# Moving the start of every large SBUF tile to a multiple of 256 bytes

## The chip, the cores and the metric

The kernel runs on one core of one Trainium2 chip. The metric is the device time of one execution in microseconds (us); lower is better. The core has a matrix engine (TensorE, PE in the rows), three elementwise engines (VectorE = DVE, ScalarE = ACT, GpSimd = POOL), an engine that here issues most transfers (SyncE = SP), and 16 DMA engines between HBM and the on-chip memory SBUF. SBUF has 128 partitions; a tile takes the same byte range in each of them, and "where a tile begins" below is its byte offset in the partition.

## The reference

A gated block on x of [8, 512, 512], in float32. A cut version:

```
xn  = layer_norm(layernorm(x)) * gamma;  ctx = layer_norm(ctx_1024) * ctx_gamma
q   = xn @ Wq (16 heads of 64);  k, v = ctx @ Wkv (one head for all)
att = softmax(where(mask == 0, -inf, q k^T / 8)) v @ Wout
ff  = (silu(xn @ Wff1[gate]) * (xn @ Wff1[a])) @ Wff2
x   = x + tanh(g_xattn) * (att + ff)
y   = layernorm(x)
o   = slot_query + attention(slot_query -> y)            # 16 slots per batch
o   = o + expert_e(layer_norm(o))                        # 16 experts, one slot each
x   = x + tanh(g_ffn) * attention(y -> o)
```

## The kernel before

The products that need precision are split. A float32 tile is kept as a high part (rounded to the matrix engine's fp32r type) and a low part (the rest), and a product is three matrix multiplies: high x high, high x low, low x high (`products`). So nearly every large multiply has the form 128x128 stationary weights, 128x512 moving rows, 512 result columns in one PSUM bank.

The program has five stages, one after the other, each with its own SBUF plan:

1. `cross_attention`, from the start to about 600 us. For each batch `b` of 8 and each pair of heads `i` of 8, TensorE runs `pair_scores(b, i)` (L619, L622), the next batch's `queries(b+1, i)` (L580, 12 multiplies), `maxima` (L598) and `pair_out(b, i)` (L632, L633, L636). At the end of each batch come the output projections `output` (L652). ScalarE makes the exponentials (`prob_hi`, `prob`), VectorE their low part (`prob_lo`, L971), GpSimd splits the finished heads (`oT_hi`, `oT_lo`).
2. `feed_forward`, to about 1650 us: `ff_up` (L1384) and `ff_down` (L1444), weights in `w1_*` and `w2_*`, rows in `ff_b*`, `ff_t*`, `u*`.
3. `slot_attention`, to about 1790 us. `score` (L2030) multiplies `A` by `yT`; `sums` (L2051) multiplies the turned probabilities `pT` by the normalised rows `yn`. Even batches use `pT_hi_even` and `pT_lo_even`, odd ones `pT_hi_odd` and `pT_lo_odd`.
4. `experts`, to about 2245 us: 16 experts' weights of 12 MiB each are streamed from HBM.
5. `token_attention`, to the end (`c_scores` L2820, `c_out` L2853).

The order of the instructions on each engine is the order in which the code issues them; there is no scheduler. SBUF places come from the order of the `mem.sbuf` calls: each tile begins where the one before it ends, so one small tile shifts all that follow. Two tiles of `gated_block`, `ident` and `gates`, and the one-number tile `many`, live for the whole program and lie below all stages. Some tiles are reserved under a plan of one stage and used by the next, so the plans must agree on every offset; that is why the filler `slot_filler` of `slot_attention` is computed from `used`, the bytes taken so far.

Which multiply takes which tile as weights is given by the order of the arguments:

```python
for w, m in products((wq_hi, wq_lo), (nT_hi, nT_lo)):                  # queries, L580
    matmul(bank[:, :], w[:, k, i * P:(i + 1) * P], m[:, k, :], ...)    # weights, moving rows
for n, (o, w) in enumerate(products((oT_hi, oT_lo), (wo_hi, wo_lo))):  # output, L652
    matmul(banks[t], o[:, i, t * P:(t + 1) * P], w[:, i, :], ...)
for a, m in products([x[...] for x in pT[b % 2]], [x[...] for x in yn]):   # sums, L2051
```

Every slice in these lines starts a multiple of 256 bytes behind its tile's start, so its position within 256 bytes is that of the tile.

Of the kernel before, what the change touches and what calls it, by code (L numbers as in the profile page):

```python
# [5 lines left out]
F32R = mybir.dt.float32r  # L6
# [5 lines left out]
P = 128  # L12
B, S, D = 8, 512, 512
KT = D // P
TT = S // P
# [4 lines left out]
SH, SD = 16, 32  # L20
HS = SH * NS
EPS = 1e-5
MASKED = -1e30


# [11 lines left out]
class Memory:  # L37
# [5 lines left out]
    def sbuf(self, name, shape, dtype=F32):  # L43
        return self.stage.enter_context(self.nc.sbuf_tensor(name, shape, dtype))
# [79 lines left out]
def several_blocks(nc, whole, taken, I, ident, gates, x1_d, x1_out_of_first, x1_stores):  # L124

    with ExitStack() as stage:
# [139 lines left out]
        def vector(dve):  # L266
# [3 lines left out]
            with dve.Fori(0, B) as b:  # L270
# [6 lines left out]
                rows_mean_var(nc, stats[:, :, :], mean[:, :], var[:, :], spread[:, :])  # L277
                nc.vector.tensor_scalar(spread[:, 0:TT], var[:, 0:TT], EPS, None, ALU.add)
                nc.vector.tensor_scalar(spread[:, TT:2 * TT], var[:, TT:2 * TT], 1 + EPS, EPS * EPS, ALU.mult, ALU.add).then_inc(dve_step, 1)
                after(dve, act_step, A + 1)  # L280
# [34 lines left out]
def cross_attention(nc, whole, taken, I, ident, gates, many, first, x1_d, xnT_d, t_d, PIECES):  # L315
# [4 lines left out]
    with ExitStack() as stage:  # L320
        mem = Memory(nc, stage, whole, taken)
# [13 lines left out]
        minus = mem.sbuf("minus", [P, P], F32R)  # L335
        first_bias = mem.sbuf("first_bias", [P, B])
        start = mem.sbuf("start", [1, B], I32)
        ones = mem.sbuf("att_ones", [1, P])
        live, dead = mem.sbuf("live", [P, P]), mem.sbuf("dead", [P, P])
        mask_i = live[:, :].bitcast(I32)  # L340
        inv_count, k_sum = (mem.sbuf(n, [P, 1]) for n in ("inv_count", "k_sum"))
# [3 lines left out]
        mv = mem.sbuf("mean_var", [P, ROWS, 2])  # L345
        spread, rstd = (mem.sbuf(n, [P, ROWS]) for n in ("spread", "rstd"))
        mean = lambda n: mv[:, n, 0:1]

        xin = mem.sbuf("xin", [P, TT, D])
        craw = mem.sbuf("craw", [P, D])  # L350
# [9 lines left out]
        q_hi = mem.sbuf("q_hi", [P, HP, S], F32R)  # L360
        q_lo = mem.sbuf("q_lo", [P, HP, S], F32R)
        MC = DH + HP
        m_rows = mem.sbuf("m_rows", [P, TT, MC])
        m_heads = mem.sbuf("m_heads", [P, S], F32R)
        prob = mem.sbuf("prob", [P, 2, S])
        prob_hi = mem.sbuf("prob_hi", [P, 2, S], F32R)
        prob_lo = mem.sbuf("prob_lo", [P, 2, S], F32R)
        inv = mem.sbuf("inv", [P, 2, S])
# [6 lines left out]
        SC, MX, OB = (pair_bank(n) for n in ("att_scores", "att_maxima", "att_out"))  # L375
# [14 lines left out]
        live_f, rank, from_end, is_first = (flag_place[:, i * B * TT:(i + 1) * B * TT].rearrange("o (b j) -> o b j", j=TT) for i in range(4))  # L390
        best, begin, several = (flag_place[:, 4 * B * TT + i * B:4 * B * TT + (i + 1) * B] for i in range(3))
        flat = lambda ap: ap.rearrange("o b j -> o (b j)")

        first_in = [mem.sem(f"first_in{t}") for t in range(2)]
        x_in, c_in, mask_in, masks_in = (mem.sem(n) for n in ("x_in", "c_in", "mask_in", "masks_in"))
# [4 lines left out]
        ident_ready, consts, bias_ready, flags_turned, firsts_ready, firsts_spread, start_ready = (  # L400
            mem.sem(n) for n in ("ident_ready", "consts", "bias_ready", "flags_turned", "firsts_ready", "firsts_spread", "start_ready"))
# [33 lines left out]
        with nc.Block() as block:  # L435
# [85 lines left out]
            def _(pe):  # L521
# [144 lines left out]
                nc.tensor.matmul(OB[0:1, 1, 0:B * TT], live_col, ident[0:B * TT, 0:B * TT], start=True, stop=True).then_inc(flags_turned, 1)  # L666
                turn_first()
                pe.wait_ge(firsts_ready, 1)
                nc.tensor.matmul(OB[:, 1, 0:B * TT], ones[:, :], flat(is_first), start=True, stop=True).then_inc(firsts_spread, 1)
                for i in range(3):  # L670
                    queries(0, i)
                turn_context(0)
# [220 lines left out]
            def _(dve):  # L893
# [10 lines left out]
                def variances(rows):  # L904
# [5 lines left out]
                    if rows[0] == 0:  # L910
                        last = nc.vector.tensor_scalar(spread[:, 0:1], var(0, 1), EPS, None, ALU.add)
                    if rows[-1] == ROWS - 1:
                        last = nc.vector.tensor_scalar(spread[:, 1:ROWS], var(1, ROWS), 1 + EPS, EPS * EPS, ALU.mult, ALU.add)
                    last.then_inc(var_ready, 1)
# [70 lines left out]
                        nc.vector.scalar_tensor_tensor(x_rows[:, t, :], out_banks(b)[t], gates[:, 0:1], x_rows[:, t, :],  # L985
                                                       ALU.mult, ALU.add).then_inc(x_added, 1)

                nc.vector.memset(ones[:, :], 1.0)
                def split_wq(k):
                    dve.wait_ge(wq_hi_done, k + 1)  # L990
                    nc.vector.tensor_tensor(wq_lo[:, k, :], raw_wq[k], plain(wq_hi[:, k, :]), ALU.subtract).then_inc(wq_lo_dve, 1)
# [815 lines left out]
def slot_attention(nc, whole, I, ident, x_stats, slot_w, weights_in, wo_in, xin, x_in, vectors, small_in, ff, x1_stored, ff_down, low_bytes, o2T, hT, x1_d, yT_d):  # L1807

    with ExitStack() as stage:
        mem = Memory(nc, stage, whole)  # L1810
# [19 lines left out]
        shift, top, nb, total, mv, *inv = (columns[:, 2 * i:2 * i + 2] for i in (0, 1, 2, 3, 5, 4, 10))  # L1830
        last_rstd, spare_col = columns[:, 22:23], columns[:, 30:31]
        sd, bv_col, stat1 = columns[:, 12:13], columns[:, 16:16 + KT], columns[:, 24:30]
        used = 4 * (B * TT * 6 + 4 * KT * D + P + 4 * B * TT + 32)
        second_pT = [mem.sbuf(f"pT_{part}_even", [P, TT, HS], F32R) for part in ("hi", "lo")]
        mem.sbuf("slot_filler", [P, (low_bytes - used) // 4 - 2 * TT * HS])

# [60 lines left out]
        flat = lambda t, i: t[:, 2 * i:2 * i + 2, :].rearrange("p t n -> p (t n)")  # L1897
# [271 lines left out]
        def statistics(first, last):  # L2169
            part = slice(first, last)  # L2170
            rows_mean_var(nc, x_stats[:, part, :], mean[:, part], var[:, part], half[:, part])
            nc.vector.tensor_scalar(var[:, part], var[:, part], EPS, None, ALU.add).then_inc(kept, 1)

# [55 lines left out]
        def vector(dve):  # L2229
# [62 lines left out]
            nc.vector.drain()  # L2292
            nc.vector.tensor_scalar(sd, mv[:, 1:2], EPS, None, ALU.add).then_inc(kept, 1)
            nc.vector.scalar_tensor_tensor(h_in[:, :], o1[:, :], mv[:, 0:1], e_gain[:, :], ALU.subtract, ALU.mult)
# [759 lines left out]
def gated_block(nc, I, out):  # L3054

    scratch = lambda name, shape: nc.dram_tensor(name, shape, F32, kind="Internal").ap()
    x1_d = scratch("x1", [B, S, D])
    xnT_d = scratch("xnT", [2, B, P, KT, S])
    t_d = scratch("ff_t_factors", [B // 2, 4, P, 2, 2, S])
    made_pieces = 12  # L3060
    with ExitStack() as whole:
        sbuf = lambda stack, name, shape: stack.enter_context(nc.sbuf_tensor(name, shape, F32))
        ident, gates = sbuf(whole, "ident", [P, P]), sbuf(whole, "gates", [P, 2])
        many = whole.enter_context(nc.sbuf_tensor("many", [1, 1], I32))

        reserved = lambda plan, name, shape: plan.enter_context(nc.sbuf_tensor(name, shape, F32R))
        HK = KT // 2 * P
        with ExitStack() as plan:
            first_raw = sbuf(plan, "ff_first_raw", [P, 2, KT * P])
            sbuf(plan, "ff_first_stats_place", [P, B * TT * 6])  # L3070
            first_w1 = reserved(plan, "ff_first_w1", [P, 2, 7, HK])
            sbuf(plan, "ff_first_other_places", [P, 2 * 2 * 7 * HK + 3 * KT * S])
            first_b = [reserved(plan, f"ff_first_b{n}", [P, 2, 2, S]) for n in ("12", "11", "21")]
            sbuf(plan, "ff_first_sums_place", [P, 2 * KT * S + 8 * S + 3 * KT * S])
            first_a21 = reserved(plan, "ff_first_a21", [P, 2, 2, HK])
        with ExitStack() as plan:
            turned_place = [plan.enter_context(nc.sbuf_tensor(f"ff_t_{n}", [P, 4, P], F32R)) for n in ("sum", "high")]
        first = FirstGroup(nc, whole, (first_raw, first_w1, first_b, first_a21), I, xnT_d)

        taken = []  # L3080
        x1_begun = cross_attention(nc, whole, taken, I, ident, gates, many, first, x1_d, xnT_d, t_d, made_pieces)
        with nc.sbuf_tensor("bo_place", [P, D], F32R) as bo_place:
            pass
        o2T = sbuf(whole, "o2T", [P, KT, P])
        with ExitStack() as until_experts:
            hT = sbuf(until_experts, "hT", [P, KT, E, B])
            with ExitStack() as until_slots:
                x_stats = sbuf(until_slots, "x_stats", [P, B * TT, 6])
                slot_w_in, slot_wo_in, slot_x_in, slot_small_in = (whole.enter_context(nc.semaphore(f"slot_{n}_in")) for n in ("weights", "wo", "x", "small"))
                with ExitStack() as place:  # L3090
                    slot_w, slot_x, slot_vectors = slot_places(nc, place, expert_low_bytes())

                def load_slot(sp, what):
                    if what == "rows":
                        load_slot_vectors(sp, I, slot_vectors, slot_small_in)
                        sp.dma_start(slot_x[:, :, :], x1_d.rearrange("b (t p) d -> b p t d", p=P)[0]).then_inc(slot_x_in, 16)
                    else:
                        for w in what:
                            sp.dma_start(slot_w[w][:, :, :], I[f"L0_ffn_d_W{w}"].rearrange("(k p) n -> p k n", p=P)).then_inc(slot_wo_in if w in "vo" else slot_w_in, 16)

                ff, x1_stored, ff_down = feed_forward(nc, whole, taken, I, gates, first, turned_place, x_stats, load_slot, x1_begun, x1_d, xnT_d, t_d, made_pieces)
                early_w, w1_in, wg_in, w2_in, bias_rows, bias_in = slot_attention(nc, whole, I, ident, x_stats, slot_w, slot_w_in, slot_wo_in, slot_x, slot_x_in, slot_vectors, slot_small_in,
                                                              ff, x1_stored, ff_down, expert_low_bytes(), o2T, hT, x1_d, xnT_d)
            early_weights = experts(nc, whole, I, ident, hT, o2T, early_w, w1_in, wg_in, w2_in, bias_rows, bias_in)
        token_attention(nc, whole, I, ident, gates, 4 * KT * E * B + expert_low_bytes(), early_weights, o2T, bo_place, x1_d, xnT_d, out)
# [23 lines left out]
```

## Time and profile before

| | |
|---|---|
| median of 3 timed runs | 2393.14 us (2392.7 to 2393.7) |
| span of the profiled execution | 2397.8 us |
| TensorE busy in it | 2126.1 us, 89% |
| VectorE / ScalarE / GpSimd busy | 1331.8 / 672.7 / 621.2 us |
| moved by DMA | 565.13 MB |
| idle time of TensorE ahead of `e_down` (experts), put down to a DMA | 82.4 us |

The profiled execution's time is its span; it is 4.7 us (0.2%) above the median of the timed runs. "Busy" counts the time from an instruction's start to its end; TensorE's multiplies overlap (each is shown with some 390 ns, and the next one starts some 230 ns after it), so the distance from start to start is the pace of a stream.

### The profile page before, as it was taken

What the parts mean: (1) busy time and instruction counts of PE and PEld (TensorE: products, weight loads), DVE (VectorE), ACT (ScalarE), POOL (GpSimd) and SP (SyncE); (2) the same over time, 40 slices, a digit from 0 to 9 for tenths busy, and PEclk for the clock granted to TensorE, in tenths of its full rate; (3) what the DMA queues carried; (4) which work ended last, traced back from release to release, by engine and by line L of the source; (5) the groups of instructions that cost most, each with busy time, mean ns of one, the idle gap of its engine ahead of it and who ended that gap; (6) DMA issues with size and microseconds to landing.
All of it is one profiled execution on the core that took longest, in us unless ns stands there. A gap on an engine that the chain in (4) does not pass through costs nothing. (4 is left out here: it accounts for less than half of the span.)

```text
span 2397.8 us, 30018 instructions
## 1 busy us (share of the span) xinstructions
PE 2126.1 (89%) x11425; PEld 1596.2 (67%) x11425; DVE 1331.8 (56%) x2112; ACT 672.7 (28%) x1066; POOL 621.2 (26%) x552
## 2 busy tenths in 40 slices
PE   6999999999989999999999999999998443644898
PEld 5677777777668778888888888887873111211577
DVE  7665666566437777666776676666651000000387
ACT  2544554455533331111111111112430000000231
POOL 5444654464458850320032000000320000000010
PEclk9899999999999999999999999998998766877899
DMA  4223223311387659664966494434879999999767
GB/s 156 77 103 124 74 78 111 129 62 62 106 313 289 240 207 385 228 219 158 360 228 219 158 369 158 158 128 157 321 283 421 427 427 428 430 426 429 285 231 261
DMA packets 182380, 565.13 MB, mean 236 GB/s; under 512 B 15304, under 2 KB 98792, under 8 KB 152392
## 3 DMA queue, kind: packets, MB, share of 16 engines
q1 hardware_dynamic: 172936, 504.37, 55.9%
q10 hardware_dynamic: 9312, 58.99, 5.9%
q8 instruction: 84, 1.38, 0.2%
q14 instruction: 48, 0.39, 0.0%
HBM read 450.07 MB, written 113.25 MB: 235 GB/s over the span
## 5 line engine op out<-in xcount | busy, mean ns | idle before, releaser
L1444 PE MATMUL ff_down<-w,u 128*128 128x512 f32 x1536 | 362.3, 394 | 8.1 <-DVE ff_x L1717 8.1
L1384 PE MATMUL ff_up<-ff_t,w 128*128 128x512 f32 x1488 | 358.9, 390 | 4.1 <-ACT ff_gate L1517 4.1
L1444 PEld LDWEIGHTS ff_down<-w,u 128*128 128x128 f32 x1536 | 290.7, 190 | 73.4 <-DVE ff_x L1717 12.9
L1384 PEld LDWEIGHTS ff_up<-ff_t,w 128*128 128x128 f32 x1488 | 280.0, 188 | 62.6 <-issue 4.5
L1717 DVE SCALAR_TENSOR_TENSOR ff_x<-ff_down,gates,ff_x 128x512 f32<-128x512 f32 x256 | 191.0, 749 | 86.8 <-PE ff_down L1444 85.1
L2500 PE MATMUL e_down<-e_w,e_ug 128*32 128x512 f32 x480 | 72.7, 760 | 185.9 <-issue 103.5
L1384 PE MATMUL ff_up<-ff_b,w 128*128 128x512 f32 x954 | 234.3, 389 | 0.0
L1384 PEld LDWEIGHTS ff_up<-ff_b,w 128*128 128x128 f32 x954 | 179.3, 188 | 37.3
L2500 PEld LDWEIGHTS e_down<-e_w,e_ug 128*32 128x32 f32 x480 | 18.2, 136 | 239.7 <-issue 151.9
L1509 ACT ACTIVATE ff_gate<-ff_gate 128x512 f32<-128x512 f32 x62 | 39.2, 633 | 410.3 <-DVE ff_gate L1693 410.3
L2608 DVE TENSOR_TENSOR e_u_rows<-e_turned,e_b1T 128x128 f32<-128x128 f32 x16 | 4.7, 292 | 264.5 <-PE e_turned L2491 264.5
L2165 POOL TENSOR_TENSOR yn_lo<-y,yn_hi 128x2048 fp32r<-128x2048 f32 x8 | 36.7, 4592 | 436.7 <-ACT yn_hi L2123 436.7
L978 DVE TENSOR_TENSOR acc<-att_out,inv 64x512 f32<-64x512 f32 x128 | 88.1, 688 | 79.8 <-ACT inv L771 78.2
L2953 POOL TENSOR_TENSOR v_pairs<-v_biased,c_odd_rows 128x512 f32<-128x512 f32 x2 | 2.5, 1286 | 496.2 <-DVE v_biased L3030 496.2
L881 POOL TENSOR_TENSOR oT_lo<-acc,oT_hi 128x512 fp32r<-128x512 f32 x64 | 116.3, 1818 | 10.0 <-issue 1.1
L580 PE MATMUL att_general<-nT_hi,wq_hi 128*128 128x512 f32 x256 | 109.2, 427 | 4.0 <-DVE q_lo L957 2.5
L1528 ACT COPY ff_gate<-ff_up 128x512 f32<-128x512 f32 x62 | 36.5, 589 | 271.3 <-PE ff_up L1384 271.3
L971 DVE TENSOR_TENSOR prob_lo<-prob,prob_hi 128x1024 fp32r<-128x1024 f32 x64 | 81.4, 1271 | 55.3 <-ACT prob L760 55.3
L93 POOL TENSOR_TENSOR ff_t_sum<-ff_t_sum,ff_t_high 128x512 f32<-128x512 f32 x20 | 28.0, 1399 | 313.1 <-DMA ff_t_high<-xnT 313.1
L767 ACT ACTIVATE inv<-att_out 64x512 f32<-64x512 f32 x128 | 75.9, 593 | 103.1 <-PE att_out L636 102.3
L580 PE MATMUL att_general<-nT_hi,wq_lo 128*128 128x512 f32 x256 | 102.9, 402 | 0.0
L580 PE MATMUL att_general<-nT_lo,wq_hi 128*128 128x512 f32 x256 | 102.5, 400 | 0.0
(449 smaller groups left out, 4308.8 us busy)
## 6 DMA issues: line engine op xcount, KB each, us to landing
w<-ff_w_factors SPq DMA_DIRECT2D x48, 1792.0 KB, 7.4
e_wg<-in_L_ffn_e_Wg SPq DMA_DIRECT2D x15, 4096.0 KB, 29.7
e_w<-in_L_ffn_e_W SPq DMA_DIRECT2D x14, 4096.0 KB, 24.2
e_w<-in_L_ffn_e_W ACTq DMA_DIRECT2D x13, 4096.0 KB, 49.8
ff_w_factors<-w SPq DMA_DIRECT2D x15, 1792.0 KB, 7.2
w<-ff_w_parts SPq DMA_DIRECT2D x48, 512.0 KB, 5.0
ff_t<-ff_t_factors SPq DMA_DIRECT2D x16, 1024.0 KB, 14.6
e_w<-in_L_ffn_e_W SPq DMA_DIRECT2D x16, 1024.0 KB, 9.9
```

The costliest lines, as they stand in the source:

```text
L580: last = nc.tensor.matmul(bank[:, :], w[:, k, i * P:(i + 1) * P], m[:, k, :], start=n == 0, stop=n == 3 * KT - 1)
L767: nc.scalar.activation(inv[halves[odd], i % 2, :], OB[halves[1 - odd], odd, :], ACT.Ln)
L881: nc.gpsimd.tensor_tensor(oT_lo[:, i, :], acc[:, i % 2, :], plain(oT_hi[:, i, :]), ALU.subtract).then_inc(o_done, 1)
L971: nc.vector.tensor_tensor(two(prob_lo[:, :, :]), two(prob[:, :, :]), two(plain(prob_hi[:, :, :])), ALU.subtract).then_inc(low_probs, 1)
L978: last = nc.vector.tensor_tensor(acc[half, i % 2, :], OB[half, odd, :], inv[half, i % 2, :], ALU.mult)
L1384: last = nc.tensor.matmul(bank[:, :], a, m, start=start and c == 0, stop=stop and c == 5)
L1444: last = nc.tensor.matmul(DN[m % 2][:, :], a, w, start=c == 0, stop=c == 5)
L1509: nc.scalar.activation(g, DN[n][:, :] if n < PLAIN else g, ACT.Silu).then_inc(gate1_done, 1)
L1528: nc.scalar.copy(gate0[n % 2][:, :], up_bank(n, A11_B11)[:, :]).then_inc(p1_kept, 1)
L1717: v.scalar_tensor_tensor(place, DN[m % 2][:, :], gates[:, 0:1], place, ALU.mult, ALU.add).then_inc(down_taken, 1)
L2165: nc.gpsimd.tensor_tensor(yn[1][:, b % 2], y[:, :, :], plain(yn[0][:, b % 2]), ALU.subtract).then_inc(yn_lo_done, 1)
L2500: last = nc.tensor.matmul(YB[q * QW:(q + 1) * QW, :], ug[:, j * Q + q, :], w2[i][:, q * J + j, :], start=j == 0, stop=j == J - 1)
```

## The change

Four small pads are added, two tiles change places, and one tile of 512 bytes is given up:

- `gated_block`: 64 bytes (`to_next_line`) after `many`; everything of all stages moves up by 64.
- `cross_attention`: `att_ones` (512 bytes) is dropped, and the ones that the prologue needs once are written into an unused part of the tile `inv`; 96 bytes (`small_to_next_line`) go before `xin`; `m_heads` (2048 bytes) now stands before `m_rows` (1152 bytes), with 128 bytes behind it.
- `slot_attention`: 128 bytes before `pT_hi_even`; the filler behind shrinks by as much.

No instruction is added, removed or moved to another place in its engine's order; sizes and counts of transfers are the same. What changes is addresses. The start of the tiles, modulo 256 bytes:

| tiles | before | after |
|---|---|---|
| attention: `wq_hi/lo`, `wkv_hi/lo`, `wo_hi/lo` | 192 | 0 |
| attention: `xin`, `craw`, `nT_hi/lo`, `cT_hi/lo`, `k_*`, `v_*`, `k_max`, `q_hi/lo` | 96 | 0 |
| attention: `m_heads`, `prob*`, `inv`, `acc`, `oT_hi/lo`, `x_rows`, `piece_*` | 224 | 0 |
| feed-forward: all large tiles | 192 | 0 |
| slots: `pT_hi_even`, `pT_lo_even` | 64 | 0 |
| slots: `A`, `yT`, `yn`, `pT_*_odd`, `d_prob`, `z` and the rest | 192 | 0 |
| experts and token attention: all large tiles | 192 | 0 |
| `ident` (whole program) | 128 | 128 |

```diff
@@ cross_attention
-        ones = mem.sbuf("att_ones", [1, P])
...
+        mem.sbuf("small_to_next_line", [P, 96 // 4])
 
         xin = mem.sbuf("xin", [P, TT, D])
...
+        m_heads = mem.sbuf("m_heads", [P, S], F32R)
         m_rows = mem.sbuf("m_rows", [P, TT, MC])
-        m_heads = mem.sbuf("m_heads", [P, S], F32R)
+        mem.sbuf("m_rows_to_next_line", [P, LINE // 2 // 4])
         prob = mem.sbuf("prob", [P, 2, S])
...
+        ones = inv[0:1, 1, 256:256 + P]
...
-                nc.tensor.matmul(OB[:, 1, 0:B * TT], ones[:, :], flat(is_first), start=True, stop=True).then_inc(firsts_spread, 1)
+                nc.tensor.matmul(OB[:, 1, 0:B * TT], ones, flat(is_first), start=True, stop=True).then_inc(firsts_spread, 1)
...
-                nc.vector.memset(ones[:, :], 1.0)
+                nc.vector.memset(ones, 1.0)
@@ slot_attention
-        used = 4 * (B * TT * 6 + 4 * KT * D + P + 4 * B * TT + 32)
+        mem.sbuf("slot_to_next_line", [P, LINE // 2 // 4])
+        used = 4 * (B * TT * 6 + 4 * KT * D + P + 4 * B * TT + 32) + LINE // 2
@@ gated_block
         many = whole.enter_context(nc.sbuf_tensor("many", [1, 1], I32))
+        sbuf(whole, "to_next_line", [P, LINE // 4 // 4])
```

## Rows read from the trace of the kernel before

**Rows 1.** The page: busy us, share of the span, instructions.
```profile
PE 2126.1 (89%) x11425; PEld 1596.2 (67%) x11425; DVE 1331.8 (56%) x2112; ACT 672.7 (28%) x1066; POOL 621.2 (26%) x552
```
**Rows 2.** Stretches of each stage: length, busy us, granted clock, DMA share, GB/s.
```profile
100.00:600.00 500.00, 493.74 (x2628) 367.53 (x2627) 312.28 (x455) 252.21 (x353) 251.47 (x216) 1.00 0.26 89
...
1050.00:1700.00 650.00, 643.81 (x2979) 533.14 (x2978) 450.30 (x705) 138.36 (x239) 56.93 (x66) 0.99 0.59 213
1700.00:1780.00 80.00, 79.90 (x437) 67.71 (x435) 54.55 (x102) 33.53 (x59) 28.79 (x7) 1.00 0.75 288
...
1850.00:2200.00 350.00, 160.29 (x1260) 57.83 (x1252) 19.27 (x68) 17.48 (x33) 0.00 (x0) 0.72 1.01 428
```
**Rows 3.** Timeline of PE, feed-forward: start us, us of the group.
```profile
902.74 2.88 PE L1384 MATMUL ff_up<-ff_t,w 128*128 128x512 f32 x12
905.46 1.52 PE L1384 MATMUL ff_up<-ff_b,w 128*128 128x512 f32 x6
```
**Rows 4.** Timeline of PE, output projections; 25 rows left out between.
```profile
304.13 0.40 PE L652 MATMUL att_maxima<-wo_hi,oT_hi 128*128 128x512 f32 x1
...
310.19 0.40 PE L652 MATMUL att_maxima<-wo_hi,oT_lo 128*128 128x512 f32 x1
```
**Rows 5.** Timeline of PE, queries; nine rows left out between.
```profile
566.86 0.39 PE L580 MATMUL att_general<-nT_lo,wq_hi 128*128 128x512 f32 x1
...
569.19 0.40 PE L580 MATMUL att_general<-nT_hi,wq_lo 128*128 128x512 f32 x1
```
**Rows 6.** Timeline of PE, weighted values; two rows left out between.
```profile
570.44 0.39 PE L633 MATMUL att_out<-prob_hi,v_lo 128*128 128x512 f32 x1
...
571.13 0.64 PE L636 MATMUL att_out<-prob_lo,v_hi 128*128 128x512 f32 x2
```
**Rows 7.** One source line, L2051: duration ns min/median/max, first and last start.
```profile
L2051 PE MATMUL slot_general<-yn_lo,pT_hi_even x32: 390/393/404, 1689.6 to 1783.5; 128*128 128x512 f32 x32
...
L2051 PE MATMUL slot_general<-yn_lo,pT_hi_odd x32: 387/389/398, 1704.7 to 1790.9; 128*128 128x512 f32 x32
```
**Rows 8.** Timeline of PE, slot scores at the lower clock; six rows left out.
```profile
1671.58 0.63 PE L2030 MATMUL slot_scores<-yT_lo,A_hi 128*128 128x512 f32 x1
...
1674.56 0.63 PE L2030 MATMUL slot_scores<-yT_hi,A_lo 128*128 128x512 f32 x1
```
**Rows 9.** Groups by line and form, PE: count, busy us, mean ns, idle before.
```profile
L1444 PE MATMUL ff_down<-w,u 128*128 128x512 f32 x1536 | 362.3, 394 | 8.1 <-DVE ff_x L1717 8.1
L1384 PE MATMUL ff_up<-ff_t,w 128*128 128x512 f32 x1488 | 358.9, 390 | 4.1 <-ACT ff_gate L1517 4.1
...
L580 PE MATMUL att_general<-nT_lo,wq_hi 128*128 128x512 f32 x256 | 102.5, 400 | 0.0
...
L652 PE MATMUL att_maxima<-wo_hi,oT_lo 128*128 128x512 f32 x128 | 50.6, 396 | 0.0
...
L633 PE MATMUL att_out<-prob_hi,v_lo 128*128 128x512 f32 x128 | 50.1, 392 | 0.0
```
**Rows 10.** Timeline: VectorE's low part and the multiply that waits for it.
```profile
313.91 1.23 DVE L971 TENSOR_TENSOR prob_lo<-prob,prob_hi 128x1024 fp32r<-128x1024 f32 x1 [2.53 <-ACT prob L760]
...
315.47 0.63 PE L636 MATMUL att_out<-prob_lo,v_hi 128*128 128x512 f32 x2
```
**Rows 11.** Waits of PE in 0 to 620 us: us in total, times, longest.
```profile
PE att_out L636 <- DVE prob_lo L971: 1.4, 5, 0.6
```
**Rows 12.** Groups by form, GpSimd and VectorE: count, busy us, mean ns.
```profile
L113 POOL TENSOR_TENSOR ff_t_sum<-ff_t_sum,ff_t_high 128x512 fp32r<-128x512 f32 x20 | 25.9, 1294 | 2.9
...
L113 POOL TENSOR_TENSOR piece_sum<-piece_sum,piece_high 128x512 fp32r<-128x512 f32 x12 | 15.5, 1294 | 0.0
...
L1717 DVE SCALAR_TENSOR_TENSOR ff_x<-ff_down,gates,ff_x 128x512 f32<-128x512 f32 x256 | 191.0, 749 | 86.8 <-PE ff_down L1444 85.1 <-DMA ff_x<-x 1.2
...
L985 DVE SCALAR_TENSOR_TENSOR x_rows<-att_maxima,gates,x_rows 128x512 f32<-128x512 f32 x16 | 11.9, 750 | 9.1 <-PE att_maxima L652 9.1
```

More of the change, by code:

```diff
@@ L22 @@
 EPS = 1e-5
+LINE = 256
 MASKED = -1e30
```

## The prediction

> **What bounds the kernel now.** I read the page's busy line first: TensorE is busy 89% of the span and no other engine over 56% [rows 1]. An average over stages hides who sets the end, so next I cut the span into stretches. In attention (100 to 600 us) TensorE is busy 493.74 of 500 us at a granted clock of 1.00, in feed-forward 643.81 of 650, in the slots 79.90 of 80. In 1850 to 2200 us, the experts, the DMA share is 1.01 at 428 GB/s and TensorE is busy under half of the time [rows 2]. So up to about 1780 us the pace of TensorE sets the time, after that the DMA engines do, and the last 150 us are mixed. Busy time says nothing about pace where instructions overlap, so the third view is the timeline of TensorE alone, from which I take the distance from start to start inside long runs of equal multiplies.
>
> **What the starts show.** All of these are 128x128 weights with 512 moving columns, at full clock.
> - Feed-forward: twelve multiplies from 902.74 to 905.46 us, so 2.72 / 12 = 226.7 ns each [rows 3]. Weights and moving rows both begin at 192 modulo 256 bytes.
> - Output projections: 26 distances from 304.13 to 310.19 us, 6.06 / 26 = 233.1 ns [rows 4]. Weights `oT` at 224, moving `wo` at 192.
> - Queries: ten distances from 566.86 to 569.19 us, 233.0 ns [rows 5]. Weights `wq` at 192, moving `nT` at 96.
> - Weighted values: three distances from 570.44 to 571.13 us, 230 ns [rows 6]. Weights `v` at 96, moving `prob` at 224.
> - The slots' sums are the best comparison, since the same line alternates between two weight tiles: with `pT_hi_even` (64, against 192 of `yn`) the median multiply lasts 393 ns, with `pT_hi_odd` (192 against 192) 389 ns, and the minima are 390 and 387 [rows 7]. A multiply's duration carries the pace here: feed-forward shows a mean of 390 where the output projections show 396 [rows 9].
>
> The reading that fits all five: a multiply is slower by 3 to 6.5 ns when its weights and its moving rows begin at different places within 256 bytes, and at the quick pace when they begin at the same place. Alignment to 64 bytes doesn't explain it, since 64 and 192 are aligned alike and `even` differs from `odd`. The queries speak against the weights alone: their weights stand at 192, as feed-forward's do, and they are slow.
>
> **The change part by part.** After it, every large tile stands at 0, so every such pair has equal places. Feed-forward, scores of the slots and the last stage had equal places before (192 and 192) and have them after: nothing moves by this reading. The terms:
> - Output projections: 768 multiplies (three products of 256; one of the groups is in [rows 9]) by 233.1 - 226.7 = 6.4 ns: 4.9 us.
> - Queries: 768 multiplies in 64 runs of 12; the first of each run is longer for another reason, so 704 by 6.3 ns: 4.4 us.
> - Weighted values: 64 pairs with six multiplies, the first again left out, 320 by 3.3 ns: 1.1 us.
> - Slots' sums of the even batches: 96 by 4 ns: 0.4 us.
>
> Sum 10.8 us, all on TensorE while it sets the pace. What could be late next is the low part of the probabilities. It ends at 313.91 + 1.23 = 315.14 us and its multiply starts at 315.47, so 0.33 us are to spare in that pair [rows 10]; TensorE arrives some 12 x 6.3 + 3 x 3.3 = 86 ns earlier after the change, which fits. Where it waits already, five times in the stage [rows 11] and in the last batch's seven pairs, whose 12 multiplies each are output projections, the gain goes into the wait: 7 x 12 x 6.4 ns = 0.5 us off. Left: 10.3 us.
>
> The other edits I cost at nothing. The ones are still one memset of 128 numbers on VectorE before the mask has come and one tiny multiply; no one else touches that part of `inv` before. The exchange of `m_heads` and `m_rows` changes no instruction. Whether elementwise engines feel a start: the same GpSimd subtraction takes 1294 ns on `piece_sum` at 224 and 1294 ns on `ff_t_sum` at 192, VectorE's addition 750 ns on `x_rows` at 224 and 749 on `ff_x` at 192 [rows 12]. They don't feel it, and they have slack.
>
> The transfers: stores and loads cover the same bytes from a start that is now at 0 instead of 192, 96 or 224. Only in the experts does their rate set the time, some 460 us at 428 GB/s [rows 2] with targets at 192. Below, nothing is gained. Above, I have no row at another start under saturation; the nearest bound is how little the rate could still rise, and I allow 1%, 4.6 us. I take 0, because the engines' share is already 1.01 and the packets are long.
>
> The Trainium skill, "DMA: Bandwidth & Descriptors", section "How a descriptor splits into AXI transactions", says that a descriptor which doesn't start at a multiple of 256 bytes begins its first read at the boundary below and pays for the bytes fetched in vain, and the same page puts the ceiling at 435 GB/s. If that charged 192 bytes to each 8 KiB written into SBUF, the rate could be 425 at best; the row's 428 is above, so here the rule doesn't reach the written side. By the ceiling alone the stage could give back at most 1.6%, 7 us.
>
> Against the profiled span of 2397.8 us the sum gives 2387.5; the timed runs lie 4.7 us below that span, and 2393.1 - 10.3 = **2382.8 us**.
>
> **The rivals.**
> - *A start at 0 is better in itself.* At the lower clock seven slot scores take 2.98 us, 425.7 ns each [rows 8], half of which is 213 ns; at full clock the quick pace is 226.7. So some 13.8 ns per multiply don't shrink with the clock and might come from the memory's side. If the start at 0 removed them, feed-forward's 4194 multiplies (five groups, two in [rows 9]) would give 58 us more: 2325 us. Against it: all pairs of equal places so far stand at one start, 192, so no row shows that the place itself matters. Chance 4%. The Trainium skill's page "TensorE: Matmul & The Clock Gate", section "Back-to-back issue gap", gives 512/2.4 + 2.5 = 216 ns for such a multiply and would put 10.7 ns instead of 13.8 here.
> - *The transfers gain too*, up to 1% of the experts: 2378 to 2382. Chance 8%.
> - *The gain is half swallowed*: VectorE's low part or GpSimd becomes late in most pairs. It decides from 0.09 us of slack down; the pair of [rows 10] has 0.33. Then 5 us are left: 2388. Chance 5%.
> - *Addresses do nothing* and the slower pace of attention comes from its traffic (elementwise engines reading the tiles beside it). Against it: `even` and `odd` alternate in the same traffic. 2393. Chance 6%.
> - *Slower*: two equal starts at 0 collide as the unequal ones do, and the quick pace belongs to 192. One pair of rows decides: if `ff_up` goes from 226.7 to 233.1 ns, its stage loses 4194 x 6.4 ns = 27 us, and attention gains nothing: 2420. The rows can't exclude it, since none has both at 0; but nothing makes 192 special. Chance 5%.
>
> **How the numbers follow.** The forecast, gain of TensorE in attention and slots, has 72%; its own range is 2380 to 2387, from 13 us (if the longer first multiplies and the narrow ones of keys and values shrink as well) down to 6 (some pairs wait). The range 2373 to 2389 adds the transfers' case, with the two terms at their upper ends together, and the swallowed half; it leaves out 4 + 6 + 5 = 15%. About 0.2% (4.8 us) is what a measurement of this kernel tells from no change. Faster by more than that: 72 + 8 + 4 and half of the swallowed case, 86%; within: 9%; slower: 5%.
>
> **What the profile after would show.** The output projections, queries and even sums at 226 to 228 ns from start to start, their means at 390; `ff_up` and `ff_down` unmoved; the start of feed-forward and all that follows some 10 us earlier; the experts' rate still 428 GB/s. The prediction is wrong if the pace of `ff_up` moves in either direction, if the output projections stay at 233, or if the feed-forward stage starts earlier and the end doesn't follow.

## The result, and the profile after

| | before | after |
|---|---|---|
| median of the timed runs, side by side | 2395.05 us (2392.7 to 2399.82, 6 runs) | 2384.22 us (2379.03 to 2389.96, 6 runs) |
| span of the profiled execution | 2397.8 us | 2387.4 us |

The ratio after to before is 0.9952, with a 95% interval of 0.9938 to 0.9966: 0.48% faster. The forecast was 2382.8 us, -0.43%. The size came out; two terms of its sum did not, as the rows show. Line numbers after are higher by three (by four from the slots on).

First the page and the windows of the kernel after (columns as in [rows 1, 2]):

```profile
PE 2120.5 (89%) x11425; PEld 1592.5 (67%) x11425; DVE 1331.9 (56%) x2112; ACT 672.7 (28%) x1066; POOL 621.9 (26%) x552
```
```profile
100.00:600.00 500.00, 493.14 (x2643) 368.84 (x2642) 313.06 (x457) 252.74 (x354) 254.92 (x220) 1.00 0.26 89
...
1850.00:2200.00 350.00, 171.68 (x1324) 61.99 (x1316) 20.16 (x72) 19.07 (x36) 0.00 (x0) 0.73 1.00 431
```

In the same 500 us of attention TensorE begins 2643 multiplies instead of 2628, and the experts' rate is 431 instead of 428 GB/s [rows 2]. The second was not forecast.

Now the timeline of TensorE in a stream of 36 output projections, which answers to [rows 4]:

```profile
299.66 0.48 PE L655 MATMUL att_scores<-wo_hi,oT_hi 128*128 128x512 f32 x1
299.97 0.40 PE L655 MATMUL att_scores<-wo_lo,oT_hi 128*128 128x512 f32 x1
...
302.51 0.39 PE L655 MATMUL att_scores<-wo_hi,oT_hi 128*128 128x512 f32 x1
...
307.73 0.39 PE L655 MATMUL att_maxima<-wo_hi,oT_lo 128*128 128x512 f32 x1
```

From 299.97 to 302.51 lie eleven distances: 2.54 / 11 = 230.9 ns. From 302.51 to 307.73 lie 23: 5.22 / 23 = 227.0 ns. So the stream reaches the quick pace, but only from about its twelfth multiply on. Before, the same stream ran at 233.1 also late in it [rows 4]. Most streams of attention aren't that long: the queries are 61 streams of 12 and one of 36, the output projections 38 of 12, six of 36, one of 24 and one of 72. A stream of queries, answering to [rows 5]:

```profile
562.54 0.50 PE L583 MATMUL att_general<-nT_hi,wq_hi 128*128 128x512 f32 x1
562.87 0.40 PE L583 MATMUL att_general<-nT_lo,wq_hi 128*128 128x512 f32 x1
...
565.18 0.39 PE L583 MATMUL att_general<-nT_hi,wq_lo 128*128 128x512 f32 x1
```

Ten distances from 562.87: 2.31 / 10 = 231 ns, against 233.0 before. The sums of the slots (answering to [rows 7]), the last of the feed-forward's sources, and the experts:

```profile
L2055 PE MATMUL slot_general<-yn_lo,pT_hi_even x32: 387/389/397, 1684.7 to 1778.4; 128*128 128x512 f32 x32
...
L2055 PE MATMUL slot_general<-yn_lo,pT_hi_odd x32: 387/389/396, 1699.8 to 1785.8; 128*128 128x512 f32 x32
```
```profile
L1387 PE MATMUL ff_up<-ff_first_b,ff_first_w x24: 389/389/470, 666.0 to 672.7; 128*128 128x512 f32 x24
```
```profile
L2484 PE MATMUL e_u<-e_w,e_h x512: 592/592/1061, 1805.9 to 2221.2; 128*32 128x512 f32 x171
```

Even and odd sums now read alike, 387/389 (before 390/393 and 387/389). In the kernel before, these starts read 671.0 for the first `ff_up`, and 1812.7 and 2231.4 for the first and the last `e_u`. So the profiled execution is 5.0 us ahead at the feed-forward stage, 6.8 at the experts and 10.2 behind them. The 5.0 at the feed-forward stage are nearly all attention's own: from the first output projection (125.0 us before, 124.8 after) to the first `ff_up` it is 546.0 us before and 541.2 after, 4.8 less. Groups by form (answering to [rows 9]):

```profile
L1447 PE MATMUL ff_down<-w,u 128*128 128x512 f32 x1536 | 363.5, 395 | 9.7 <-DVE ff_x L1720 9.7
L1387 PE MATMUL ff_up<-ff_t,w 128*128 128x512 f32 x1488 | 357.7, 389 | 2.4 <-ACT ff_gate L1520 2.4
...
L583 PE MATMUL att_general<-nT_lo,wq_hi 128*128 128x512 f32 x256 | 101.4, 396 | 0.0
...
L655 PE MATMUL att_maxima<-wo_hi,oT_lo 128*128 128x512 f32 x128 | 50.0, 391 | 0.0
```

The projections' mean fell from 396 to 391, the queries' only from 400 to 396, and `ff_up` stands where it stood.

### The profile page after: what moved, and what is told of

Same layout as the page of the kernel before. It is cut to its first block and busy times, and to the rows that moved or that the text cites. A ratio compares the mean times of both kernels' runs of the same rounds, so it can differ in the third digit from the quotient of the medians.

```text
span 2387.4 us, 30018 instructions
## 1 busy us (share of the span) xinstructions
PE 2120.5 (89%) x11425; PEld 1592.5 (67%) x11425; DVE 1331.9 (56%) x2112; ACT 672.7 (28%) x1066; POOL 621.9 (26%) x552
```

## The experiments

Two theories were open behind the result: equal places pay for all of it (10.3 us), and the quicker transfers are chance; or the gain has two halves, one from equal places, one from transfers whose SBUF side begins at 0.

### The kernel after once more (e0)

No edit; it sets how well a difference can be told.

> The changed kernel once more, beside the two parts of it. Theory A (matrix multiplies and transfers both gain): the gap to the kernel before is again about 10 us, of which 5 are gained by the end of attention and 3 or more in the experts' stretch. Theory B (only the multiplies gain, the rest of the 10 us was chance in the experts' stretch): about 5 to 6 us over the repeated runs, ratio 0.9975.

Measured: 2385.22 us (6 runs) against 2396.41 (23 runs), ratio 0.9958 (0.9943 to 0.9972). The gain stands: 10 to 11.5 us. Its profiled execution is 6.7 us ahead at the first `ff_up`, but 2.1 of that before the first output projection, which starts at 122.9 us instead of 125.0; from there on it is 4.6. Start-ups scatter, and the granted clock goes with it: it is 0.95 in the first 100 us of e0 and e2 (first output projection at 122.9 and 123.3 us) and 0.90 or 0.91 in the other three (124.8 to 126.0). So the milestones of one profiled run don't divide the gain to better than 2 us.

### Equal places, but at 192 (e1)

```diff
 # the kernel after, in gated_block
-        sbuf(whole, "to_next_line", [P, LINE // 4 // 4])
```

> The changed kernel without the 64 bytes of to_next_line: all large tiles, those of attention and of the even sums too, begin at 192 modulo 256, so places are equal but not 0. If equal places are what the multiplies want, attention ends 5 us earlier than before, as with 0, and the settled output projections run at 226.7 ns; if the multiple of 256 matters, they stay near 233 ns. If transfers gain from a start at 0, the experts' stretch stays at 428 GB/s here and the kernel is 4 to 5 us slower than the changed one (about 2388); if not, both are the same.

Measured: 2390.76 us (12 runs), ratio 0.9979 (0.9969 to 0.9989): half of the gain, 5.0 us. The windows of e1, its sums, and the second part of a stream of 36 output projections:

```profile
1850.00:2200.00 350.00, 166.22 (x1308) 60.73 (x1304) 19.77 (x71) 18.48 (x35) 0.00 (x0) 0.72 1.01 428
```
```profile
L2055 PE MATMUL slot_general<-yn_lo,pT_hi_even x32: 387/389/397, 1689.3 to 1782.9; 128*128 128x512 f32 x32
```
```profile
306.32 0.39 PE L655 MATMUL att_scores<-wo_hi,oT_hi 128*128 128x512 f32 x1
...
311.53 0.39 PE L655 MATMUL att_maxima<-wo_hi,oT_lo 128*128 128x512 f32 x1
```

The 23 distances of the stream are 5.21 / 23 = 226.5 ns; over the whole stage the output projections' mean distance is 228.6 ns and the queries' 230.6 (229.3 and 230.7 after). The sums are as quick as with 0/0 too, while the experts' rate is back at 428. So the place itself is nothing to TensorE, and it is something to the transfers. e1 keeps the other edits of the change (the ones inside `inv`, the exchanged tiles); no run has these alone, but the paces leave them little to explain. In its profiled execution attention, from the first output projection on, gains only 1.8 us: its waits are longer (below), and the granted clock is 0.98 from 100 to 300 us where it was 1.00 before. The timed runs carry the verdict here, not that execution.

### The 64 bytes alone (e2)

```diff
 # the kernel before, in gated_block: later stages at 0,
 # attention still unequal (0, 160 and 32), pT_even at 128
+        sbuf(whole, "to_next_line", [P, 64 // 4])
```

> The kernel before with 64 bytes more at the bottom and nothing else: feed-forward, slots (but the even probabilities, at 128) and experts begin at 0, attention stays unequal (0, 160 and 32). Multiplies alone: no gain, attention's output projections at 233 ns, 2393 to 2395 us. If a transfer's start matters: the experts' stretch at 431 GB/s and 4 to 5 us faster than before.

Measured: 2391.39 us (12 runs), ratio 0.9981 (0.9970 to 0.9993): the other half, 4.6 us (1.7 to 7.2). Attention's streams keep 233 ns: from the 13th to the 36th multiply of a stream, 5.36 / 23 = 233.0. The stream and the windows:

```profile
301.88 0.40 PE L652 MATMUL att_scores<-wo_hi,oT_hi 128*128 128x512 f32 x1
...
307.24 0.40 PE L652 MATMUL att_maxima<-wo_hi,oT_lo 128*128 128x512 f32 x1
```
```profile
1850.00:2200.00 350.00, 171.93 (x1352) 62.43 (x1348) 20.14 (x72) 19.06 (x36) 0.00 (x0) 0.73 1.01 432
```

0.21% + 0.19% = 0.40%, beside 0.48% and 0.42% for both edits together: the halves add up within their intervals, and the theory that equal places pay for all falls. The granted clock differs a little from run to run (0.939 to 0.947). A fit of the 59 timed runs listed with their clock, which takes the clock as a second variable, still gives 5.8 us for e1 and 4.2 for e2, each within some 2 us. The records of the DMA packets say how the transfers gain (a packet is one contiguous piece that one DMA engine moves; 1830 to 2190 us, over all packets of a size):

```
kernel   starts   8 KiB packets: median   32 KiB packets: median   GB/s
before   192      312 ns                  1216 ns                  428.9
e1       192      312 ns                  1216 ns                  427.4
after    0        309 ns                  1213 ns                  431.2
e0       0        309 ns                  1213 ns                  430.6
e2       0        309 ns                  1213 ns                  430.9
```

A packet is 3 ns shorter in the median whatever its length, so the price is per packet and not per byte. In the mean it is 4.1 to 4.8 ns (8 KiB 313.5 to 309.4, 32 KiB 1217.9 to 1213.1, before and after), because off the line the durations also spread upward: a tenth of the 8 KiB packets take 319 ns or more there, and 309 at 0. With some 558 packets an engine in these 360 us that is 2.4 us, 0.7%, as the rate says: its mean rises from 428.2 to 430.9, 0.6%. Over some 450 us in which the rate sets the time that makes 2.9 us of e2's 4.6.

The length of this stretch in one profiled execution doesn't show it. From the first to the last `e_u` (the rows x512) it is 418.7 us before, and 415.3, 414.4 and 413.2 in after, e0 and e2, but 413.7 in e1 as well, at 428 GB/s. So part of the 3.4 us that the profiled execution after gains there is chance; the packets' durations and the timed runs carry the point.

### Pairs of places, alone on the core (m1)

This kernel computes nothing of the reference: TensorE runs a head of 12 and a tail of 36 multiplies for each of 14 pairs of places, parted from the next pair by multiplies of 64 rows, with no other engine or transfer at work.

```diff
+PAIRS = [("a", 0, 0), ("b", 192, 192), ("c", 96, 96), ("d", 192, 96), ("e", 224, 192), ("f", 64, 192), ("g", 96, 224),
+         ("h", 0, 128), ("i", 0, 64), ("j", 0, 32), ("k", 0, 16), ("l", 0, 4), ("m", 4, 4), ("n", 128, 128)]
```

> A kernel that computes nothing of the reference (it copies x to out): streams of 48 multiplies, 128x128 weights by 512 columns of fp32r, each ahead of them four multiplies with 64 rows, with weights and moving rows at chosen places modulo 256, 14 pairs of places, three times over. Equal places (0/0, 192/192, 96/96, 128/128, 4/4): the last 36 at 226.7 ns each, the first 12 at about 230, since a stream takes some eleven multiplies to settle. Unequal ones (192/96, 224/192, 64/192, 96/224, 0/128, 0/64, 0/32): 233 ns throughout. Open: 0/16 and 0/4, whether the grain is 256, 64, 16 or 4 bytes. The rival (attention's slower pace comes from other engines' traffic) expects 226.7 ns in all of them, since nothing else runs here.

Its timeline, six of the tails (the three repeats of a tail agree to 0.01 us):

```profile
38.78 8.32 PE L55 MATMUL tail<-x_a,w_a 128*128 128x512 f32 x36
50.56 8.32 PE L55 MATMUL tail<-x_b,w_b 128*128 128x512 f32 x36
...
74.14 8.60 PE L55 MATMUL tail<-x_d,w_d 128*128 128x512 f32 x36
...
134.34 8.41 PE L55 MATMUL tail<-x_i,w_i 128*128 128x512 f32 x36
...
170.34 8.73 PE L55 MATMUL tail<-x_l,w_l 128*128 128x512 f32 x36
182.62 8.69 PE L55 MATMUL tail<-x_m,w_m 128*128 128x512 f32 x36
```

Equal places at 0, 96, 128 and 192 all take 8.32 us; unequal ones 8.50 to 8.60, which is 5 to 8 ns for each multiply, except 0/64, where it is 2.5. The effect needs no traffic, so the rival of the elementwise engines' traffic is out. Two things no theory had: 4/4 is equal and takes 8.69, so a start at 4 costs by itself (nothing between 4 and 16 was run); and the heads of 12 hardly differ, 2.99 to 3.06 us with equal places and 3.02 to 3.08 with unequal ones (3.11 and 3.12 with a start at 4).

### How long a stream takes to settle (m3)

Also nothing of the reference: four pairs, each in sixteen runs of 12 parted by two multiplies of 64 rows (`cut`), sixteen runs that only change the bank (`turn`), sixteen parted by a wait on VectorE (`late`), and 192 in a row (`long`).

```diff
+for n in range(16):
+    stream(("cut_a", "cut_b")[n % 2], name, 12)
+    halves(name)
+for n in range(16):
+    stream(("turn_a", "turn_b")[n % 2], name, 12)
+for n in range(16):
+    stream("late", name, 12).then_inc(asked, 1)
+    pe.wait_ge(told, ...)
+stream("long", name, 192)
```

> This kernel computes nothing of the reference; it runs multiplies of 128x128 weights by 512 moving columns alone on TensorE, for four pairs of places (0/0, 192/192 equal; 192/96, 224/192 unequal), in four forms: sixteen runs of 12 parted by two multiplies of 64 rows, sixteen runs of 12 that only change the bank, sixteen runs of 12 parted by a wait on VectorE, and 192 multiplies in a row. Theory (equal places give the quick pace only in a stream that has settled, about eleven multiplies after a break): in the row of 192, unequal pairs take 192 x 6.5 ns = 1.25 us more than equal ones; in runs of 12 after the half-row multiplies only 12 x 2 to 4 ns = 25 to 50 ns a run, 0.4 to 0.8 us for the sixteen. A change of bank alone is no break, so there the full 16 x 12 x 6.5 ns = 1.25 us are expected. For the wait I expect the behaviour of the half rows. Rival (each multiply gains its 6.4 ns wherever it stands, and attention lost its gain in waits): 1.2 us for the sixteen runs in every form. Rival (only the bank's change or the start of a sum breaks the stream): the second form behaves as the first.

Its timeline, the first multiplies of the forms and the whole `long` groups, for 0/0 (a) and 192/96 (d):

```profile
18.12 2.88 PE L58 MATMUL cut_a<-x_a,w_a 128*128 128x512 f32 x12
...
72.02 1.20 PE L58 MATMUL turn_a<-x_a,w_a 128*128 128x512 f32 x4
...
167.12 43.86 PE L58 MATMUL long<-x_a,w_a 128*128 128x512 f32 x192 [0.19 <-DVE to_line L48]
...
403.51 2.96 PE L58 MATMUL cut_a<-x_d,w_d 128*128 128x512 f32 x12
...
458.33 3.08 PE L58 MATMUL turn_a<-x_d,w_d 128*128 128x512 f32 x12
...
555.56 45.25 PE L58 MATMUL long<-x_d,w_d 128*128 128x512 f32 x192 [0.19 <-DVE to_line L48]
```

The `cut` form lasts until `turn` begins: 72.02 - 18.12 = 53.90 us at 0/0 and 458.33 - 403.51 = 54.82 at 192/96. All forms, 192 multiplies each:

```
            0/0     192/192   192/96   224/192
cut        53.90    53.91     54.82    54.62
turn       43.65    43.65     45.09    44.90
late       51.46    51.46     52.15    52.02
long       43.69    43.67     45.08    44.91
```

In `long` and `turn` unequal places cost 1.2 to 1.4 us, 6.4 to 7.5 ns a multiply; in `cut` 0.7 to 0.9, in `late` 0.6 to 0.7. Behind half-row multiplies the mean distances of an equal run are 331, 233, 232, 230, 231, 229 and then 227 ns; at 224/192 they are 330 and then 235, 232, 235, 232 to the end. So a break takes a third to a half of the gain of a run of 12 (0.9 of 1.4 us are left in `cut` at 192/96, above the expected 0.4 to 0.8; 0.6 to 0.7 in `late`), and a change of bank takes none. The rival in which each multiply gains wherever it stands falls.

### Transfers by the place in SBUF (m2, m4, m5)

None of the three computes anything of the reference. Each issues rounds of 2 MiB transfers, four in flight, waits for them, and marks the round by a tiny memset whose name holds the kind and a letter for the place.

```diff
+place = bufs[i][:, o // 4:o // 4 + 4096]        # o: start modulo 256
+sp.dma_start(place, ...)                        # read, long: 16 KiB runs
+sp.dma_start(place.rearrange(...), ...)         # short: eight pieces of 2 KiB
+sp.dma_start(scratch[e], place)                 # write: store to HBM
 # m2: places 0, 192, 96, 64, 16, 4;  m4: 0, 128, 32, 192;  m5: 192, 0, 128, 0
```

> A kernel that computes nothing of the reference (it copies x to out at the end): eight transfers of 2 MiB, 16 KiB in each partition, up to four under way, from HBM into SBUF and then as many from SBUF into HBM, with the SBUF side at 0, 192, 96, 64, 16 and 4 modulo 256 bytes, three times over. If a load's start matters as the experts' stretch suggests (431 against 428 GB/s), a round at 0 takes 0.7% less than one at 192: 0.3 us of 39. If it doesn't, 0, 192, 96 and 64 agree within 0.1 us. For stores, where SBUF is read, a read that begins at the boundary below would cost up to 2% at 192. At 16 and 4 a start inside 32 bytes may cost one more beat per packet, 0.4%.

m2 measured, between two marks (8 transfers): loads at 0 41.49 and 41.55 us, at the other five places 41.70 to 41.94; stores at 0 40.58, 41.20 and 41.25, at the others 40.89 to 41.26, nearly all 40.9. I read this as "loads gain 0.3 us, stores nothing". The expected 2% for stores at 192, and an extra price at 16 and 4, didn't show.

> This kernel computes nothing of the reference; it loads 16 x 2 MiB a round, four transfers in flight, to starts 0, 128, 32 and 192 modulo 256 bytes, once as 16 KiB runs of each partition (long) and once as eight pieces of 2 KiB (short); each round is marked by a small memset. Theory A (a load whose target doesn't start at 0 pays a fixed price at the edge of each packet): long rounds at 128, 32 and 192 take 2 x 0.3 = 0.6 us more than at 0 of some 81 us, and short rounds, with four times as many packets, about 2.4 us more. Theory B (the price is by the bytes, since every line of 256 bytes is split): 0.6 us more in both forms. Theory C (only loads at 0 differ, 128 is as good as 0, because the unit is 128 bytes or less): the round at 128 equals that at 0. If the differences vanish, the gain in the experts was not one of targets.

m4's marks (16 transfers a round; in brackets VectorE's idle time before the mark, which is the round):

```profile
765.20 0.07 DVE L57 MEMSET long_at_a<- 128x8 f32 x1 [80.30 <-SPq L44]
846.07 0.07 DVE L57 MEMSET long_at_b<- 128x8 f32 x1 [80.80 <-SPq L44]
...
1095.53 0.07 DVE L57 MEMSET short_at_a<- 128x8 f32 x1 [86.86 <-SPq L44]
1186.83 0.07 DVE L57 MEMSET short_at_b<- 128x8 f32 x1 [91.24 <-SPq L44]
1278.31 0.07 DVE L57 MEMSET short_at_c<- 128x8 f32 x1 [91.41 <-SPq L44]
1369.73 0.07 DVE L57 MEMSET short_at_d<- 128x8 f32 x1 [91.36 <-SPq L44]
```

16 KiB runs cost 0.5 us more off the line (up to 1.3 in single rounds), 2 KiB pieces 4.4 us more (5%), and 128 is no better than 32 or 192. The price is per packet. This run's theory A is right in kind, but its 2.4 us counted four times as many packets; the records have eight times as many, 16384 of 2 KiB against 2048 of 16 KiB, and eight times 0.5 to 0.6 us are 4 to 4.8. But the round at 0 had always been the first of its kind, which m5 mends.

> This kernel computes nothing of the reference. In the two transfer kernels before, the round at 0 was always the first of its kind, right after a round of another kind, so its order and its place could not be told apart. Here the four rounds of a kind stand at 192, 0, 128, 0, with eight transfers of 2 MiB each; kinds are loads in 16 KiB runs (long), loads in 2 KiB pieces (short), and stores (write). Theory (the start of a load's target decides): long b and d take about 0.3 us less than long a and c of some 41.7 us, short b and d about 2.2 us less than short a and c, and the four store rounds agree but for the first, which follows another kind. Rival (the order decides: the first round of a kind is the quick one for loads and the slow one for stores): long a and short a are the quick ones, and b equals c equals d. A start at 0 that costs stores something would show in write b and d at 0.3 us more than write c.

m5's marks, second repeat (a and c off the line, b and d at 0):

```profile
601.32 0.07 DVE L60 MEMSET long_at_b<- 128x8 f32 x1 [41.37 <-SPq L47]
643.14 0.07 DVE L60 MEMSET long_at_c<- 128x8 f32 x1 [41.76 <-SPq L47]
...
732.89 0.07 DVE L60 MEMSET short_at_a<- 128x8 f32 x1 [48.06 <-SPq L47]
778.74 0.07 DVE L60 MEMSET short_at_b<- 128x8 f32 x1 [45.78 <-SPq L47]
826.79 0.07 DVE L60 MEMSET short_at_c<- 128x8 f32 x1 [47.98 <-SPq L47]
...
954.06 0.07 DVE L60 MEMSET write_at_b<- 128x8 f32 x1 [40.48 <-SPq L47]
994.97 0.07 DVE L60 MEMSET write_at_c<- 128x8 f32 x1 [40.85 <-SPq L47]
1035.51 0.07 DVE L60 MEMSET write_at_d<- 128x8 f32 x1 [40.47 <-SPq L47]
```

The start decides, not the order: short pieces take 45.8 us at 0 and 48.0 off it. And my reading of m2's stores was wrong: stores too gain 0.37 us, 0.9%. The packets of m2 had said so, 611 ns at 0 and 614 to 615 at the other five places. Why two of its three store rounds at 0 were slow all the same isn't shown. They stood first of their kind, behind loads, but m5's first store round, behind short loads, took no longer than its third (40.87 and 40.85 us in the second repeat). (One long round at 0, in the third repeat, took 41.93 and so showed no gain; the other five took 41.37 to 41.56.) By the packets' records a 2 KiB load lasts 88 ns off the line and 84 at 0, a 16 KiB store 615 and 611.

## Why the prediction was right, and where its sum was not

**The total** held: -10.3 us forecast, -0.48% and -0.42% measured (11.5 and 10.1 us). That is luck in part: 10.3 us stood for multiplies whose measured gain is 6.1, and the transfers, which stood at nothing, were worth 4.6 (1.7 to 7.2).

**"A multiply ... at the quick pace when they begin at the same place"**: right as a mechanism (e1, m1), and it holds without traffic. The size of the terms failed. I took the pace of feed-forward's long streams [rows 3] for runs of 12. From the start-to-start distances under 300 ns of all streams, before and after:

| term | forecast | mean distance | measured |
|---|---|---|---|
| output projections, 768 | 6.4 ns: 4.9 us | 233.1 to 229.3 | 3.8 ns: 2.9 us |
| queries, 704 | 6.3 ns: 4.4 us | 234.0 to 230.7 | 3.3 ns: 2.3 us |
| weighted values, 320 | 3.3 ns: 1.1 us | 231.6 to 230.0 | 1.6 ns: 0.5 us |
| even sums, 96 | 4 ns: 0.4 us | 232.5 to 228.7 | 3.8 ns: 0.4 us |

The sum is 6.1 us instead of 10.8. m3 shows the cause: behind a half-row multiply or a wait, an equal run needs some six to eleven multiplies until it settles, and that takes a third to a half of the gain of a run of 12. The weighted values' 3.3 ns came from three distances of one pair [rows 6]; all of them together show half of it. [rows 5] could have warned: I left out the first multiply of each run "for another reason" and took the rest as settled.

**"-0.5 us of waits"**: neither shown nor excluded. The wait on `prob_lo` is 1.4 us in five pairs before [rows 11] and 1.3 in four after, but 2.3 in six and seven pairs of e0 and e1, and 1.0 in three of e2. All distances over 435 ns up to the first `ff_up` add up to 40.7 us before and 40.8 after, 40.8 in e2, 42.6 in e0 and 45.4 in e1. So the execution after lost nothing to waits, and equal ones scatter by more than the term. e1's timed 5.0 us (2.6 to 7.4) fit 6.1.

**"I take 0"** for the transfers is the step that failed, with its reason ("the engines' share is already 1.01 and the packets are long"). A share of 1.01 says that the engines are never idle, not that their packets can't get shorter; each got 3 ns shorter. The case "the transfers gain too" had 8%, and its bound of 1% was good: 0.6% by the rate, 4.6 us (1.7 to 7.2) by e2. Where e2's part beyond the experts' 2.9 us lies stays open: within its interval it may be nothing, or the loads and stores of the stages before.

**The rule on how a descriptor splits.** I concluded that it "doesn't reach the written side". The runs show otherwise: loads off the line pay per packet, and so do stores. A rate of 428 above 425 excluded the full charge of 192 bytes, not a smaller price. The Trainium skill, "DMA: Bandwidth & Descriptors", section "How a descriptor splits into AXI transactions", has a read that doesn't start at a multiple of 256 bytes begin at the boundary below and pay for the bytes between there and the start. The unit of 256 bytes agrees with the runs (128 is as bad as 32, m4). The charge by the bytes does not: stores, which read SBUF, last 614 to 615 ns a packet at 4, 16, 64, 96 and 192 alike (m2), against 611 at 0, and loads to these places agree within 0.2 us of 41.8.

**The rivals.** "A start at 0 is better in itself" and "slower: two equal starts at 0 collide" fall with `ff_up` at 389 ns as before and with 8.32 us at 0/0 and 192/192 in m1. "Addresses do nothing" falls with m1. "Half swallowed": the multiplies did give little more than half (6.1 of 10.8), but by short streams, not by a late VectorE.

**What the profile would show**: `ff_up` unmoved, right; even sums at 226 to 228, nearly (228.7, where the odd ones stood before); projections and queries at 226 to 228, only in long streams; feed-forward 10 us earlier, wrong (5.0); the experts at 428 GB/s, wrong (431).

## What to carry to other kernels

Put large tiles at a multiple of 256 bytes of the partition. In this kernel it cost a few pads, and in these runs it was worth two separate things: some 4 ns for each DMA packet (under 1% of a saturated stream of long packets, 5% with 2 KiB pieces), and 6 to 7.5 ns of 233 for each multiply of a long stream whose weights and moving rows stood at unequal places (2.5 with 0 and 64), about half of that in attention's runs of 12. When you read a pace from a long stream, don't apply it to short ones; and when a resource's share reads 1.0, ask what a single unit of its work costs before you call it fixed.

When rounds are compared, let no case always stand first of its kind, and read the single packets beside the rounds: m2's stores misled me by their rounds, not by their packets.

## What was not expected of the hardware

- A stream with equal places settles at 226.7 ns only after some six to eleven multiplies behind a multiply of 64 rows or a wait; a change of PSUM bank doesn't break it (m3).
- Of unequal places 0/64 is the mildest (2.5 ns), and 4/4 is slow though equal (10 ns a multiply, m1).
- A packet's price for a start off the 256-byte line is a fixed 3 to 4 ns, on loads of 2, 8 and 32 KiB and on stores of 16 KiB (84 to 88, 309 to 312, 1213 to 1216, 611 to 615 ns). Loads of 16 KiB are the exception: in m5 their median stays at 611 off the line and the mean of those under 630 ns goes from 611.0 to 612.6, while their rounds mostly lengthen by 0.3 to 0.4 us. Where the rest of that price lies no run here shows.
- Elementwise engines still don't feel the place: GpSimd's subtraction on `piece_sum` takes 1293 ns and VectorE's addition 749 on both `ff_x` and `x_rows`, as in [rows 12].
